# A three-layer interaction tower on one core: another bank for one set of sums, one turning moved, one slot's units reordered

## What is computed

```python
e = jnp.stack([tbl_0[ids[:, 0]], ..., tbl_31[ids[:, 31]]], axis=1)   # (1024, 32, 16)
x0 = xk = e
outs = []
for W in (W0, W1, W2):                    # (32, 32, 64), (32, 64, 64), (32, 64, 64)
    xk = relu(einsum('bmd,bhd,mhk->bkd', x0, xk, W))
    outs.append(sum(xk, axis=2))
h = concatenate([*outs, dense_ctx], axis=1)                          # (1024, 208)
h = maximum(h @ W_top1 + b_top1, 0)                                  # 512 wide
h = maximum(h @ W_top2 + b_top2, 0)                                  # 256 wide
y = h @ W_top3                                                       # (1024, 1)
```

## Time and profile before

| what | value |
|---|---|
| median of 3 runs | 631.56 us |
| the profiled execution's own time | 631.58 us |
| its span | 629.8 us |
| TensorE's mean granted clock | 1.0 of full speed |
| VectorE busy | 587.4 us, 93% |
| TensorE busy | 586.5 us, 93% |
| GpSimd busy | 436.0 us, 69% |
| ScalarE busy | 370.1 us, 59% |
| share of the chain that ended last | VectorE 52%, TensorE 25%, issue 11% |

### The profile page before, as it was taken

The page is one execution under the profiler, slowest core; times in us unless marked ns, Lnnn a source line. Parts: engine busy times, 40 slices in busy tenths (PEclk is TensorE's granted clock), DMA queues, the critical chain, the costliest instruction groups (busy, mean ns, idle before and its releaser), DMA issues.

```text
span 629.8 us, 8255 instructions
## 1 busy us (share of the span) xinstructions
PE 586.5 (93%) x3046; PEld 220.1 (35%) x3046; DVE 587.4 (93%) x354; ACT 370.1 (59%) x638; POOL 436.0 (69%) x412
## 2 busy tenths in 40 slices
PE   0787898899999989999999999999999999999998
PEld 0344432232323323333333333333334333334355
DVE  2289998999999999999999999999999999999994
ACT  0146554847576665757576575757576575737561
POOL 6777874588979788886888588886888592603012
DMA  6667493968392828567391938557391937500000
GB/s 174 187 189 241 153 315 90 305 172 293 67 339 51 279 96 215 199 134 279 70 344 30 260 126 191 223 135 279 67 345 28 255 134 206 208 1 1 0 1 1
DMA packets 33076, 105.19 MB, mean 167 GB/s; under 512 B 8902, under 2 KB 16076, under 8 KB 29196
## 3 DMA queue, kind: packets, MB, share of 16 engines
q1 hardware_dynamic: 24012, 102.18, 51.3%
q0 software_dynamic: 8192, 2.11, 2.7%
q10 hardware_dynamic: 832, 0.38, 0.3%
HBM read 88.90 MB, written 15.73 MB: 166 GB/s over the span
## 4 chain that ended last, share of the span: by engine, by line
DVE 52%; PE 25%; issue 11%; DVEq 0%; ACT 0%
DVE prod L632 52%; PE acca L766 8%; PE accb L766 7%; PE acc L707 2%; PE spread L813 2%; PE accb L791 1%; PE acc L791 1%; PE spread L808 1%; PE spread L809 0%; PE acc L737 0%; PE acca L791 0%; PE spread L691 0%; PE accb L843 0%; PE spread L817 0%; PE accb L836 0%
## 5 line engine op out<-in xcount | busy, mean ns | idle before, releaser
L469 POOL DMA_INDIRECT emb<-in_table,idx x256 | 247.1, 965 | 84.5 <-issue 67.9
L766 PE MATMUL acca<-prod,w 128*64 128x512 f32 x960 | 214.4, 594 | 1.4 <-DVE prod L632 0.7
L766 PE MATMUL accb<-prod,w 128*64 128x512 f32 x896 | 202.0, 596 | 12.4 <-DVE prod L632 12.3
L632 DVE TENSOR_TENSOR prod<-rows,x1a 128x2048 f32<-128x2048 f32 x64 | 145.7, 2281 | 8.0 <-ACT x1a L932 3.6
L632 DVE TENSOR_TENSOR prod<-rows,x1b 128x2048 f32<-128x2048 f32 (+1 forms) x65 | 145.8, 2247 | 1.3 <-PE accb L766 0.7
L632 DVE TENSOR_TENSOR prod<-rows,x2b 128x2048 f32<-128x2048 f32 x64 | 145.6, 2280 | 1.3 <-ACT x2b L940 1.3
L632 DVE TENSOR_TENSOR prod<-rows,x2a 128x2048 f32<-128x2048 f32 x64 | 145.6, 2279 | 0.0
L766 PEld LDWEIGHTS acca<-prod,w 128*64 128x64 f32 x960 | 67.3, 137 | 134.1 <-issue 126.4
L766 PEld LDWEIGHTS accb<-prod,w 128*64 128x64 f32 x896 | 61.3, 137 | 145.5 <-issue 105.1
L487 POOL TENSOR_TENSOR prod<-rows,mates 128x1024 f32<-128x1024 f32 x39 | 92.1, 2378 | 4.5 <-DMA rows<-field_dram 4.3
L978 ACT ACTIVATE x1a<-acc 64x512 f32<-64x512 f32 x58 | 33.1, 570 | 88.2 <-PE acc L707 86.3
(11 more groups left out here) (106 smaller groups left out, 367.1 us busy)
## 6 DMA issues: line engine op xcount, KB each, us to landing
rows<-field_dram SPq DMA_DIRECT2D x30, 2048.0 KB, 9.5
field_dram<-zb_field SPq DMA_DIRECT2D x30, 256.0 KB
mates<-field_dram SPq DMA_DIRECT2D x15, 512.0 KB, 4.5
across<-field_dram SPq DMA_DIRECT2D x52, 128.0 KB
emb<-in_table,idx POOLq DMA_INDIRECT x256, 4.9
field_dram<-zb_field SPq DMA_DIRECT2D x30, 128.0 KB
rows<-field_dram SPq DMA_DIRECT2D x4, 768.0 KB, 7.3
field_dram<-zb_field SPq DMA_DIRECT2D x15, 192.0 KB
```

Of the source, the lines that this page charges most:

```text
L469: pool.indirect_dma_start(out=emb[q % EMBS][:, j * EMB:(j + 1) * EMB], out_offset=None, in_=table, in_offset=bass.IndirectOffsetOnAxis(ap= ...
L632: nc.vector.tensor_tensor(prod[:, n % RING, t:t + count, :], of_rows, xs, ALU.mult).then_inc(s_prod, 1)
L766: mm = nc.tensor.matmul(acc[j % 2][side * HID:(side + 1) * HID, :], (w1 if layer == 1 else w2)[:, step, :], prod[:, (made(layer, s, half, ...
```

## The change

1. `sums_alone`: the sums of (1,1), layer 1 of period 0's second half, are put into the second half (256 columns) of the bank `spread`, whose first half holds the turned fields, and no longer into `acc[0]`. TensorE waits, before the first of them, for ScalarE's copy of the fields of period 1, no longer for its reads of (1,0)'s sums; (2,1) in `acc[0]` waits for those reads instead of for the reads of (1,1)'s sums; the turning of period 2 waits for the reads of (1,1)'s sums.
2. ScalarE makes `first_input(1, 1, 1)` two places sooner, right behind `first_input(1, 1, 0)`.
3. The turning of period 3 stands behind the third pair of slot 2 (`FIELDS_AT`) and no longer within layer 0 of period 2. ScalarE copies these fields out ahead of `input2(2, 0)` and no longer behind it.
4. Slot 3 opens on VectorE with both units of half 0 of (2,2), then both of (1,4); half 1 alternates as before.
5. Four matmuls of `keep_busy` instead of two behind slot 2.

```diff
--- before.py
+++ after.py
@@ -113,6 +113,9 @@
             a, b = b, a
         if j == SUBS - 1:
             return [(*stream, half, u) for stream in (a, b) for half in range(2) for u in range(UNITS)]
+        if j == FIRST_SLOT + 1:
+            return ([(*stream, 0, u) for stream in (a, b) for u in range(UNITS)] +
+                    [(*stream, 1, u) for u in range(UNITS) for stream in (a, b)])
         return [(*stream, half, u) for half in range(2) for u in range(UNITS) for stream in (a, b)]
 
     MADE = FIRST_UNITS + [unit for j in range(FIRST_SLOT, SUBS) for unit in vector_units(j)]
@@ -134,7 +137,7 @@
 
     SQUARES = L0
     ALONE0 = [t for t in EARLY_TILES if t not in LAYER0_TILES]
-    FIELDS_AT = {}
+    FIELDS_AT = {(FIRST_SLOT, 2): 3}
     SUM0 = {(FIRST_SLOT, 3): [(k, 2) for k in range(EARLY)]}
     for q in range(4, PERIODS):
         FIELDS_AT[2 * q - 5, 3] = q
@@ -310,7 +313,7 @@
 
         def sums_alone(layer, s):
             if s < FIRST_SLOT:
-                return acc[1] if (layer, s) == (2, 0) else acc[0]
+                return {(2, 0): acc[1], (1, 1): spread[:, 2 * P:]}.get((layer, s), acc[0])
             return acc0 if s % 2 else acc[1]
 
         def last_group(g):
@@ -774,11 +777,13 @@
                 n = made(layer, s, half, u) - 1
                 pe.wait_ge(s_prod, n + 1)
                 if (half, u) == (0, 0):
-                    if s == 0:
+                    if (layer, s) == (2, 1):
+                        pe.wait_ge(s_x2[1], 1)
+                        pe.wait_ge(s_z2, 1)
+                    elif (layer, s) == (1, 1):
+                        pe.wait_ge(s_field, turned_by(1))
+                    elif s < FIRST_SLOT:
                         pass
-                    elif s == 1:
-                        pe.wait_ge(s_x2[1], layer)
-                        pe.wait_ge(s_z2, layer)
                     elif s % 2 == 0:
                         pe.wait_ge(s_x2[1], SUBS - 1)
                     else:
@@ -869,6 +874,8 @@
             for k in order0(1):
                 layer0(k, 1)
                 if k == 1:
+                    pe.wait_ge(s_x2[1], 2)
+                    pe.wait_ge(s_z2, 2)
                     turn_fields(2, 0)
             for unit in FIRST_UNITS[-HELD:]:
                 outer_alone(*unit)
@@ -893,11 +900,8 @@
                         turned += 1
                     for k, q in SUM0.get((j, i), []):
                         layer0(k, q)
-                        if (k, q) == (1, EARLY_PERIODS - 1):
-                            turn_fields(EARLY_PERIODS, towers)
-                            turned += 1
                     if (j, i) == (FIRST_SLOT, 2 * UNITS - 1):
-                        keep_busy(acc[1][:, :], 2)
+                        keep_busy(acc[1][:, :], 4)
             last_tower(len(TOWER) - 1, turned)
 
         @block.scalar
@@ -1076,9 +1080,9 @@
             first_input(2, 0, 0)
             fields_out(1)
             first_input(1, 1, 0)
+            first_input(1, 1, 1)
             first_input(2, 0, 1)
             first_z(1, 0)
-            first_input(1, 1, 1)
             first_z(0, 1)
             act.wait_ge(s_top, 6 * 16)
             first_input(2, 1, 0)
@@ -1092,8 +1096,8 @@
             input1(2, 1)
             input1(3, 1)
             z1(1)
+            fields_out(3)
             input2(2, 0)
-            fields_out(3)
             input1(4, 0)
             for j in range(FIRST_SLOT + 1, SUBS):
                 if j > FIRST_SLOT:
```

## The result

The changed kernel takes 628.00 us, the median of 5 runs (627.65 to 628.35), against 631.56 for the kernel before (5 runs, 630.90 to 631.83): ratio 0.9941, 95% interval 0.9930 to 0.9952. It is faster by 3.56 us, where the sum gave 2.73; the forecast was 628.85. Its profiled execution took 628.0 us, span 626.2.

What follows compares the result with a forecast made beforehand. VectorE's chain of units was taken to set the end, with two stops to remove. From 631.58 us, -1.36 - 2.08 + 0.71 = -2.73 gave 628.85 us; range 628.0 to 630.3.

Steps and rivals of the forecast that it cites:

- The first stop: VectorE waits at unit 9, (1,1,1,0), for ScalarE's copy x2b; 1.36 us lost, all to be removed.
- rival C: Slot 3's seventh unit meets no new stop; full 3.44 us gained, 628.14 us; chance 0.07.
- Edit 1: Sums' bank and ScalarE's order: x2b of (1,1) ready at 52.4, wanted at 55.24; saves 1.36 us.
- Edit 2: Turning of period 3 moved behind slot 2's third pair: free there, x1a ready at 105.6, row loads earlier.
- the second stop: VectorE waits at 107.63 for ScalarE's x1a; 2.08 us lost, all to be removed.
- What follows slot 3: Period 4's last gathers land by 121 to 122 with the loads' end; its turning at 124.1 doesn't wait.
- Edit 3: Two layer-2 units first in slot 3: saves 2.08 us, costs 0.71 us ahead of the seventh unit.
- The new stop: VectorE waits ahead of slot 3's seventh unit for a ring slot freed by TensorE's second pair; 0.71 us.
- Edit 4: Four stand-ins for two behind slot 2 take at most 3.96 us, over before the first pair; cost nothing.
- Rival E: TensorE's clock falls to 1.2 GHz in slot 3; four slow pairs add 10.6 us, 639.4 us; chance 0.03.
- Rival A: Period 4's last gathers still take 6.07 us though loads are gone; gain 1.38, 630.20 us; chance 0.14.
- Rivals B and D: B: one stop or half of each stays, 630.2 us, chance 0.06; D: time given back, 630.5 to 631.6, 0.08.

Runs made afterwards that it cites:

- e6: Changed kernel with two `keep_busy` stand-ins behind slot 2 instead of four; 630.29 us, ratio 0.9961 to the kernel before.
- e11: Changed kernel with only the sums' bank, its waits and ScalarE's order kept, all else undone; 630.32 us, ratio 0.9971 to the kernel before.
- e2: Changed kernel with the turning of period 3 back in layer 0 of period 2; 658.12 us, ratio 0.9926, where the kernel before took 661.15.
- e13: Changed kernel with the turning of period 3 back in layer 0 of period 2, run again; 630.51 us, ratio 0.9974 to the kernel before.
- e14: Changed kernel with slot 3's units in the old alternating order, run again; 629.30 us, ratio 0.9961 to the kernel before.
- e3: Changed kernel with slot 3's units in the old alternating order; 656.02 us, ratio 0.9918, where the kernel before took 661.15.
- e4: Changed kernel again, nothing altered; 653.44 us, ratio 0.9873, where the kernel before took 661.15.
- e15: Changed kernel again, nothing altered, in a later call; 628.66 us, ratio 0.9948 to the kernel before.
- e7: Changed kernel with no `keep_busy` stand-ins behind slot 2; 630.81 us, ratio 0.9986 to the kernel before.
- e8: Changed kernel again, nothing altered; 628.16 us, ratio 0.9942 to the kernel before.

## Why the prediction was right and where it was wrong

**The first stop, and with it "-1.36": the step that failed.** "The chain loses **1.36 us**" took the length of a stop from one execution as a property of the kernel. The stop ends where ScalarE's list ends it, at T1 + 10.84, and begins where VectorE arrives, at T0 + 25.34; both ends hang on gathers, and in the profile that was read their distance was at its least. Over the 13 profiles the term is 2.02 us in the mean, 1.76 over the three of the kernel before. The sum with 2.02 is -2.02 - 2.08 + 0.71 = -3.39, against 3.56, 3.71 and 3.30 measured in three comparisons. That the changed kernel began with T0 at 29.08 and not 29.88 is the same thing seen from one pair of profiles: the old kernel would have waited the 0.80 us away at unit 9, the new one keeps it. "The median of the runs, 631.56, is the same within 0.02" made the error hard to see: the kernel before has that time whatever T0 is, as long as T1 stays. That 628.00 comes out at the low end of the range is no credit to the prediction: that end was set for rival C, which did not come.

**Edit 1: right.** Unit 9 starts without a stop, also where T1 - T0 is 16.81 (e6). e11 measures edit 1 by itself, 75.21 us from the fifth unit to slot 4, where 76.59 - 1.36 = 75.23 was to come. (2,1)'s units start without a wait, and the new waits cost nothing.

**Edit 2: the place right, its worth elsewhere.** The turning is free at 94.65, the listing starts early, the loads end at 120. But the step credits the earlier x1a to it, and with the new order x1a isn't late even without it (e2 and e13 have no stop there, 24.17 us in e2 as with it). Edits 2 and 3 overlap there: edit 2 with the old order leaves 1.24 us of the second stop (e14), the new order leaves none, with edit 2 or without. What edit 2 buys is the early end of the row loads: "What follows slot 3" has it in the right order, with the gathers landing with the loads' end. e13 shows what its absence costs.

**Edit 3: right.** The new stop was put at 0.71 us and is 0.60 by the row, 2.87 us from start to start (112.18 to 115.05) instead of 2.20, so 0.67. The pitch of 2.20 us and a pair's end decide, as worked out: rival C did not come. The order is worth 0.64 us by the stretches of e3 and e4, 0.57 by those of e14 and e15, since without it 1.24 us of the second stop stays.

**Edit 4: "nothing" was wrong in its reason, not in the sum.** The two added stand-ins lie beside other work and take no time, but they are no idle detail: without them TensorE waits 2.64 us, behind which the clock fell in the profile of e6, and slot 4 opened 1.63 us later behind the fifth unit. (The median grew by 2.13 us, and part of that can be the start-up's own fall.) Rival E, priced at +10.6 us for four slow pairs, is a real mechanism in this slot. It did not come with four stand-ins, which leave 0.93 us to wait, and where it comes (e6) it costs 1.60 us of VectorE's time in stops and not 10.6: the clock is back at 1.00 two windows later, within the three pairs.

**Rival A** (gathers late though the loads are gone) did not come: issued by 119.06, they had landed by 123.18. Under load, in e13, the last one took 6.23 us (119.37 to 125.60), as the 6.07 before. The Trainium skill, "DMA: Bandwidth & Descriptors", section "Queues, rings and completion order", has each engine take turns between its queues packet by packet. By that alone a small gather would come through in the middle of the loads; in e13, as in the kernel before, it became usable only as they ended. The price put on A, 1.35 us, is about what e13's executions at a mean clock of 1.0 lost (1.42). It was too low for the others, where the wait brought the slow clock with it: e13's profile lost 3.28 us behind slot 4's opening.

**Rivals B and D** did not come: no part of either old stop is left, and behind slot 4 the two profiles agree within 0.01 us.

**What stays open.** The means of T0 and T1 are known only through one profile per kernel, so the 0.4 us between the three comparisons isn't split further. By totals alone e11 leaves 1.99 us of the first comparison's 3.56 to edits 2 to 4, where the prediction has 1.37 for them; its profile has nothing that they could take beyond the second stop, so this is put down to scatter, not shown. Two of e15's six executions have a mean granted clock of 0.997 and took 629.59 and 629.89 us, the others 627.42 to 628.82: the changed kernel too has falls of the clock at times, and no profile of it shows where.

## What to carry to other kernels

The length of a stop is the difference of two times; find what sets each, and if these are two transfers, look at more than one execution before the length goes into a sum, since a kernel that no longer waits there also gains what its beginning had to spare. An edit that is free in the timeline can still be what keeps a later wait short: take it away in an experiment before calling it nothing. And where an edit makes TensorE's wait longer, price the slow matmuls behind it as well as the wait, and look at many executions: here the same kernel had both outcomes.

## What the hardware did that was not expected

- The granted clock fell to 0.50 behind waits of TensorE of 2.04 us (e13), 2.64 us (e6) and 4.56 us (e7), and to 0.51 in the start-up of e6 behind 1.83 us. It stayed at 1.00 behind 1.77 us, and in the start-up behind 2.26 us (e8) and 2.54 us (e11). So the length of the one wait didn't settle it. In e6 seven of 12 executions of one and the same kernel have a mean granted clock below 1.0, and they are the seven long ones. The Trainium skill, "TensorE: Matmul & The Clock Gate", section "Why this matters for your kernels", warns of longer pauses than those of e13 and e6; here shorter ones were at times enough.
- The clock's return came soon: 0.50 in one window of 2 us, then 0.65 (e13) or 0.88 (e6), then 1.00.
- The landing of a few small gathers in the start-up moves by 1.6 us between executions of like kernels (T0 28.66 to 30.25). The kernel before hid it: its own time less T1 is the same within 0.08 us in three profiles, with T0 from 29.30 to 29.88.
